# Transformer block with attention and experts: the first two stages reordered over three DMA queues

## What is computed

```python
s = layernorm(attention(xn) + bo + xn) * gamma + beta      # 16 heads of 16
# scores = (q k^T + rel_q + rel_k) / sqrt(D); rel_q, rel_k from a table of distances
y = xn + n1 + (n1 @ mix_w + mix_b);  n1 = layernorm(xn)*g1+be1
g = silu(y + sum of the best two of 8 experts on layernorm(y)*g2+be2)
```

## Time and profile before

| | |
|---|---|
| median of 3 runs | 2211.05 us (2209.01 to 2214.07) |
| the profiled execution | 2215.61 us, its span 2213.7 us |
| mean granted clock of PE | 0.869 |
| `project` | 0 to 165.6 us |
| `route` | 165.6 to 464.5 us |
| `experts` | 464.5 to 1494.3 us |
| `attention` | 1494.3 to 2213.7 us; PE busy 589.5, DVE 546.9, ACT 532.2 us |

### The profile page before, as it was taken

One profiled execution on the slowest core, in us unless ns is written; L12 is line 12 of the kernel. 1 busy time (PEld: TensorE's weight loads), 2 busy tenths in 40 slices (PEclk: granted clock), 3 DMA queues, 4 the chain that ended last, 5 costly groups with the idle time before them and its releaser, 6 DMA issues. The chain is left out here.

```text
span 2213.7 us, 32508 instructions
## 1 busy us (share of the span) xinstructions
PE 1652.7 (75%) x11192; PEld 1210.2 (55%) x11192; DVE 1144.9 (52%) x2980; ACT 1020.5 (46%) x2057; POOL 664.0 (30%) x711
## 2 busy tenths in 40 slices
PE   5536353027889788987989798976898998899881
PEld 2213133026777677876777687863555555555550
DVE  5722636503333244443323344435888888888870
ACT  3534110012434233333433234326878878888870
POOL 2560025821111111111111111105206446437435
PEclk9767575568999899999999899987999999999995
DMA  4445474778899999998999999969989899899851
GB/s 158 128 138 154 139 248 119 209 193 252 289 302 316 313 330 309 321 303 281 308 283 314 334 322 308 312 231 332 304 262 303 278 324 314 264 327 315 277 173 38
DMA packets 247731, 576.91 MB, mean 261 GB/s; under 512 B 40016, under 2 KB 86608, under 8 KB 246160
## 3 DMA queue, kind: packets, MB, share of 16 engines
q1 hardware_dynamic: 204160, 426.81, 58.0%
q0 software_dynamic: 43408, 148.04, 21.3%
HBM read 371.27 MB, written 203.42 MB: 260 GB/s over the span
## 5 line engine op out<-in xcount | busy, mean ns | idle before, releaser
L953 DVE TENSOR_TENSOR rel_out<-rl,rel_tile 128x1024 f32<-128x1024 f32 x256 | 307.5, 1221 | 240.7 <-PE rl L1005 169.9
L1220 ACT ACTIVATE scores<-scores,row_least 128x512 f32<-128x512 f32 x512 | 365.6, 717 | 25.1 <-DVE row_least L1253 24.5
L1253 DVE CUSTOM_DVE_ANT_1 scores<-sc,rq 128x512 f32<-128x512 f32 x512 | 336.7, 687 | 36.5 <-issue 35.2
L930 ACT COPY rel_tile<-rl 128x1024 f32<-128x1024 f32 x256 | 249.5, 1017 | 228.6 <-PE rl L1005 195.6
L1354 PE MATMUL pt<-ident,scores 128*128 128x128 f32 x2048 | 328.6, 285 | 30.8 <-DVE probsT L1259 15.9
L1026 PE MATMUL up<-rowsT,w 128*128 128x256 f32 x1280 | 326.5, 400 | 3.5 <-DMA w<-in_w 3.5
L1039 PE MATMUL dn<-w,hid 128*128 128x256 f32 x1280 | 326.2, 400 | 0.0
L938 ACT ACTIVATE hid<-up,b 128x256 f32<-128x256 f32 x320 | 134.1, 470 | 390.9 <-PE up L1026 390.2
L1354 PEld LDWEIGHTS pt<-ident,scores 128*128 128x128 f32 x2048 | 256.3, 147 | 105.6 <-DVE probsT L1259 52.9
L1026 PEld LDWEIGHTS up<-rowsT,w 128*128 128x128 f32 x1280 | 241.0, 199 | 32.1 <-issue 3.9
L1039 PEld LDWEIGHTS dn<-w,hid 128*128 128x128 f32 x1280 | 241.8, 199 | 28.4
(11 more groups left out here) (182 smaller groups left out, 1735.7 us busy)
## 6 DMA issues: line engine op xcount, KB each, us to landing
scratch_rel<-rel_out SPq DMA_DIRECT2D x256, 512.0 KB, 8.6
rq<-scratch_rel SPq DMA_DIRECT2D x256, 512.0 KB, 5.9
w<-in_w POOLq DMA_DIRECT2D x80, 1024.0 KB, 11.0
krows_sb<-scratch_stack SPq DMA_DIRECT2D x768, 64.0 KB, 5.3
scratch_parts<-part SPq DMA_DIRECT2D x96, 128.0 KB
by_head<-scratch_parts SPq DMA_DIRECT2D x16, 768.0 KB, 5.8
scratch_stack<-by_row SPq DMA_DIRECT2D x4, 3072.0 KB, 22.9
qrows_sb<-scratch_stack SPq DMA_DIRECT2D x192, 64.0 KB, 8.6
```

The lines of the kernel that those rows point to most:

```text
L930: nc.scalar.copy(both[:, :, u * UN:(u + 1) * UN], rl[r][:].rearrange("p a (b l) -> p l (a b)", l=TILE)).then_inc(s_kc, 1)
L953: nc.vector.tensor_tensor(out[n % SRING][:], rl[r][:].rearrange("p a (b s) -> p (a b) s", s=TILE), both[:, u * UN:(u + 1) * UN], ALU.add). ...
L1220: nc.scalar.activation(sm[j][:, i], sm[j][:, i], ACT.Exp, bias=least[:, j, i:i + 1], scale=-1.0, accum_out=es[:, g // 2 % 2, i, 2 * j + g ...
L1253: nc.vector.tensor_tensor_reduce(sm[j][:, i].rearrange("p (c s) -> p c s", c=LT), sc[i % 2][:].rearrange("p (c s) -> p c s", c=LT), rq[j][ ...
```

## The change

- `project`: the ring of parts has three places. ACT makes only part 0; `rest` works per output `c` on DVE straight from PSUM (add the bias, subtract part 0), and PE may reuse the output when `rest` has read it. DVE's normalization is cut into `statistics`, `roots`, `applied` and `second_scale`, which alternate with the rests; the tables are split last. PE turns batch 0 first and makes the constants after the products of batch 0. POOL no longer adds `bo` or `cvec`. SP stores plain `xn` and loads four small tables for `route`.
- `route`: `va` is stored from ACT's queue and `x1` from POOL's, SP keeps loads and stores of the repacking. POOL adds `cvec` to `xn` (`shifted`). DVE clears `va`. The copies alternate: ACT has (0, 0), (0, 2), (0, 4), (0, 6), (1, 0), (1, 3), (1, 6), DVE the nine others; those of the second half stand behind `place_pair(3)` on DVE and behind `exponents(3)` on ACT. The first stack store stands behind the loads (1, 0) and (1, 1) on SP.
- `experts`: the eight query pieces of the first row of tiles are requested one at a time, each ahead of a key piece.
- `attention`: `xo` is reloaded from plain `xn`, and `bo` is added by a product of a row of ones with `bo`, one more call per 128 rows.

```diff
+PRING = 3
+ZRING = 2
...
+        qk = [sb(f"qk_rest{i}", [P, 4, S]) for i in range(2)]
+        part = [[sb(f"part{i}_{k}", [P, 4, S], BF16) for k in range(PARTS)] for i in range(PRING)]
...
+            sp.dma_start(keep["tri"][:], t["tri"]).then_inc(s_ahead, 16)
+            sp.dma_start(keep["rw"][:], t["router_w"].rearrange("(k p) n -> p k n", p=P)).then_inc(s_ahead, 16)
+            sp.dma_start(keep["first_row"][:], t["first_row"].partition_broadcast(P)).then_inc(s_ahead, 16)
+            sp.dma_start(keep["turn_no"][:], t["turn_no"].partition_broadcast(P)).then_inc(s_ahead, 16)
+
+            def store_xn(b):
+                sp.wait_ge(s_xn, b + 1)
+                sp.dma_start(t["xn"][b * S:(b + 1) * S].rearrange("(p t) e -> p t e", t=ST), xn[:, b * ST:(b + 1) * ST]).then_inc(s_xs[b], 16)
+
+            store_xn(0)
+            store_xn(1)
             for b in range(B):
-                par = b % 2
-                sp.wait_ge(s_xb, b + 1)
-                sp.dma_start(t["xnbo"][b * S:(b + 1) * S].rearrange("(p t) e -> p t e", t=ST), xb[par][:]).then_inc(s_xs[par], 16)
                 for k, done in enumerate((s_p0, s_p1, s_p2)):
                     sp.wait_ge(done, 4 * (b + 1) if k == 0 else b + 1)
                     for c in range(4):
                         at = b * H + (c % 2) * (H // KC)
                         dst = t["parts"][c // 2 * PARTS + k, :, at:at + H // KC].rearrange("d h s -> h d s")
-                        sp.dma_start(dst, part[par][k][:, c]).then_inc(s_ps[par], 16)
-            for i in range(2):
-                sp.wait_ge(s_xs[i], 16 * B // 2)
-                sp.wait_ge(s_ps[i], 16 * 4 * PARTS * B // 2)
+                        sp.dma_start(dst, part[b % PRING][k][:, c]).then_inc(s_ps[b % PRING], 16)
+                if b + 2 < B:
+                    store_xn(b + 2)
+            sp.wait_ge(s_ahead, 16 * 4)
+            for b in range(B):
+                sp.wait_ge(s_xs[b], 16)
+            for i in range(PRING):
+                sp.wait_ge(s_ps[i], 16 * 4 * PARTS * len(range(i, B, PRING)))
 
         @block.gpsimd
...
             for b in range(B):
-                par, own = b % 2, slice(b * ST, (b + 1) * ST)
-                pool.wait_ge(s_vec, 2)
-                pool.wait_ge(s_xn, b + 1)
-                after(pool, s_xs[par], 16 * (b // 2))
-                nc.gpsimd.tensor_tensor(xb[par][:], xn[:, own], over_tiles(bo[:], ST), ALU.add).then_inc(s_xb, 1)
                 pool.wait_ge(s_p1, b + 1)
-                after(pool, s_ps[par], 16 * 4 * PARTS * (b // 2))
-                nc.gpsimd.tensor_tensor(part[par][2][:], qk[par][:], part[par][1][:], ALU.subtract).then_inc(s_p2, 1)
-                pool.wait_ge(s_t, (b + 1) * KC)
-                pool.wait_ge(s_xb, b + 1)
-                nc.gpsimd.tensor_tensor(xn[:, own], xn[:, own], over_tiles(cvec[:], ST), ALU.add).then_inc(s_xc, 1)
+                after(pool, s_ps[b % PRING], 16 * 4 * PARTS * (b // PRING))
+                nc.gpsimd.tensor_tensor(part[b % PRING][2][:], qk[b % 2][:], part[b % PRING][1][:], ALU.subtract).then_inc(s_p2, 1)
...
-            def take_products(b):
-                par = b % 2
-                for c in range(4):
-                    act.wait_ge(s_qk, b * 4 + c + 1)
-                    if c == 0:
-                        after(act, s_p2, b - 1)
-                    nc.scalar.activation(in_order(qk[par][:, c]), by_row(prod[c][:]), ACT.Identity, bias=bqk[:, c:c + 1]).then_inc(s_q32, 1)
-                    if c == 0:
-                        after(act, s_ps[par], 16 * 4 * PARTS * (b // 2))
-                    nc.scalar.activation(in_order(part[par][0][:, c]), by_row(prod[c][:]), ACT.Identity, bias=bqk[:, c:c + 1]).then_inc(s_p0, 1)
+            def first_part(b, c):
+                dst = part[b % PRING][0][:, c].rearrange("e (p t) -> e p t", t=ST)
+                act.wait_ge(s_qk, b * 4 + c + 1)
+                if c == 0:
+                    after(act, s_ps[b % PRING], 16 * 4 * PARTS * (b // PRING))
+                nc.scalar.activation(dst, in_order(prod[c][:]), ACT.Identity, bias=bqk[:, c:c + 1]).then_inc(s_p0, 1)
 
             def second_part(b):
-                act.wait_ge(s_r, b + 1)
-                nc.scalar.copy(part[b % 2][1][:], qk[b % 2][:]).then_inc(s_p1, 1)
+                act.wait_ge(s_r, 4 * (b + 1))
+                nc.scalar.copy(part[b % PRING][1][:], qk[b % 2][:]).then_inc(s_p1, 1)
 
             take_turned(0)
             for b in range(B):
-                take_products(b)
+                first_part(b, 0)
+                first_part(b, 1)
+                if b:
+                    second_part(b - 1)
+                first_part(b, 2)
                 if b + 1 < B:
                     take_turned(b + 1)
-                if b:
-                    second_part(b - 1)
+                first_part(b, 3)
             second_part(B - 1)
...
+            def rest(b, c):
+                turned = prod[c][:].rearrange("e (t p) -> e p t", t=ST)
+                dve.wait_ge(s_p0, 4 * b + c + 1)
+                if c == 0:
+                    after(dve, s_p2, b - 1)
+                nc.vector.scalar_tensor_tensor(qk[b % 2][:, c].rearrange("e (p t) -> e p t", t=ST), turned, bqk[:, c:c + 1],
+                                               part[b % PRING][0][:, c].rearrange("e (p t) -> e p t", t=ST),
+                                               ALU.add, ALU.subtract).then_inc(s_r, 1)
...
+            statistics(0, 0)
+            statistics(0, 1)
+            roots()
+            applied(0, 0)
+            applied(0, 1)
+            second_scale(0)
+            dve.wait_ge(s_wqk, 16 * 3)
+            for p in range(B // 2):
+                more = p + 1 < B // 2
+                rest(2 * p, 0)
+                if more:
+                    statistics(p + 1, 0)
+                rest(2 * p, 1)
+                if more:
+                    statistics(p + 1, 1)
+                rest(2 * p, 2)
+                rest(2 * p, 3)
+                if p == 0:
+                    dve.wait_ge(s_once, 1)
+                    nc.vector.tensor_tensor(cvec[:], once[:, 0], rows[:, 0], ALU.add).then_inc(s_vec, 1)
+                    nc.vector.tensor_tensor(bo[:], once[:, 1], rows[:, 1], ALU.add).then_inc(s_vec, 1)
+                if more:
+                    roots()
+                rest(2 * p + 1, 0)
+                if more:
+                    applied(p + 1, 0)
+                rest(2 * p + 1, 1)
+                rest(2 * p + 1, 2)
+                if more:
+                    applied(p + 1, 1)
+                rest(2 * p + 1, 3)
+                if more:
+                    second_scale(p + 1)
             dve.wait_ge(s_tabs, 16 * 3)
             split_table(tabq, 0)
-            rest(4)
             split_table(tabk, 1)
-            for b in range(5, B):
-                rest(b)
 
...
+            turn(0)
             pe.wait_ge(s_wqk, 16 * 3)
-            turn(0)
             for b in range(B):
-                products(b)
+                for c in range(3):
+                    product(b, c)
                 if b + 1 < B:
                     turn(b + 1)
+                product(b, 3)
+                if b == 0:
+                    pe.wait_ge(s_w, 16 * 5)
+                    pe.wait_ge(s_setup, 2 + KC)
+                    for i, w in enumerate((mix, wo)):
+                        for k in range(KC):
+                            last = nc.tensor.matmul(once[:, i], spread[:, i, k], w[:, k], start=(k == 0), stop=(k == KC - 1))
+                    last.then_inc(s_once, 1)
...
+        BY_DVE = ((0, 1), (0, 3), (0, 5), (0, 7), (1, 1), (1, 2), (1, 4), (1, 5), (1, 7))
+        BY_ACT = tuple((half, b) for half in range(2) for b in range(B) if (half, b) not in BY_DVE)
+
+        def repack_done(eng, half, b):
+            if (half, b) in BY_DVE:
+                eng.wait_ge(s_bd, BY_DVE.index((half, b)) + 1)
+            else:
+                eng.wait_ge(s_ba, BY_ACT.index((half, b)) + 1)
...
+            for b in range(B):
+                load(0, b)
             load(1, 0)
             load(1, 1)
-            store_back(4)
-            store_back(5)
-            store_back(6)
-            store_back(7)
+            store_rows(0)
             for b in range(2, B):
                 load(1, b)
             store_rows(1)
-            for i in range(2):
-                sp.wait_ge(s_vs[i], 16 * B // 2)
-            sp.wait_ge(s_x1, 16 * B)
             sp.wait_ge(s_bs, 16 * LT)
...
+            def shifted(b):
+                own = slice(b * ST, (b + 1) * ST)
+                nc.gpsimd.tensor_tensor(xn[:, own], xn[:, own], over_tiles(cvec[:], ST), ALU.add).then_inc(s_xc, 1)
+
+            def store_x1(b):
+                pool.wait_ge(s_x2, (b + 1) * ST)
+                pool.dma_start(t["x1"][b * S:(b + 1) * S].rearrange("(p t) e -> p t e", t=ST), xn[:, b * ST:(b + 1) * ST]).then_inc(s_x1, 16)
+
+            for b in range(B):
+                shifted(b)
+                if 1 < b < 6:
```

(82 more changed lines are left out.)

175 lines of the change are left out of this document (65 added, 110 removed).

## The result

| | before | after | forecast |
|---|---|---|---|
| median | 2210.03 us (4 runs) | 2177.52 us (4 runs, 2170.55 to 2181.86) | 2114 (2075 to 2160) |
| profiled execution | 2215.61 us, span 2213.7 | 2177.89 us, span 2176.3 | |
| `project` | 165.6 | 128.2 | 106 |
| `route` | 298.9 | 290.2 | 265 |
| `experts` | 1029.8 | 1020.7 | 1017 |

A forecast was written before the change was run, and what follows sets the result against it. The first two stages were taken as bound by order and waits, with no engine full. Project -60, route -34, experts -13 and attention +10 made -97 us, giving a median of 2114 us, range 2075 to 2160.

The forecast's parts named there:

- four signs of being wrong: `project` over 120 us, `rest` over 1 us beside POOL, `route` ending on POOL instead of the stores, attention over 15 us longer.
- Project, start: PE's first product in `project` at 17 us instead of 24.54, 7.5 us earlier, with the constants behind batch 0.
- Project, pace: 9.3 us per batch in `project`, 74 for eight; bounds 8.7 and 12.5.
- rival 1: POOL and DVE block each other in `project`: pace 12.5, stage 132, total 2140; chance 0.27 shared by three rivals.
- Project, end: Last rest, second and third part, four stores and landing in `project` take 13.5 us, with the table splitting hidden beside them.
- Rival 6: No change in time, which would need the front stages to be bound by transfers; chance 0.02.
- Route, until the first stack store: In `route`, first slots at T+64, third at T+157, first stack stores out at T+162, counted from the stage's start.
- Route, stack landing: In `route`, the first stack stores take 28 us to land, at T+190.
- rival 2: In `route`, stack store pairs take 34 us, loads 10 instead of 5.8; total 2139; chance 0.27 shared by three rivals.
- Route, end: `route` ends with its stack stores at T+265; POOL's path, clearings 9 us then 15 more, ends just under, at T+261.
- Experts: At the start of `experts`, spreading query requests between key pieces shortens PE's wait: -13 us (-20 to -4).
- Attention: 32 bias calls of two PE instructions, about 0.23 us each, cost 0 to 15 us in `attention`; taken as +10.

The follow-up runs named there:

- the mend: POOL's third part of batches 0, 2 and 4 also waits until the next pair is normalized, against the changed kernel; ratio 0.9813 to the kernel before, `project` 117.9 us.

## Why the prediction was right or wrong

The mechanisms that the change was built on came. The profiled stages together exceed the forecast ones by 59 us, and 47 of these lie in `project` and `route`. The steps that failed there are the overlap of POOL's third part with DVE's normalization, which the sum put at nothing, and POOL's path at the end of `route`, which it took too short. Three of the four signs of being wrong came too: `project` over 120 us, the end of `route` on POOL, and attention over 15 us longer. The fourth, `rest` at over 1 us beside POOL, did not.

- **Project, start:** right. First product at 16.6 us, forecast 17. Of this the constants' move is worth 3 us, the turning's the rest.
- **Project, pace:** this step failed. The prediction asked of `rest` whether POOL blocks it, and answered rightly that it doesn't. It did not ask the same of the second piece of DVE work that the change puts beside POOL's third part, the normalization, which reads and writes SBUF. There the four instructions took 5.1 us instead of 1.4, with PE and ACT in a chain behind them. That is the mechanism of rival 1. That its price of 12.5 us per batch lies so near the 12.2 measured is luck: it counted 4.1 us of blocked DVE in every batch, but 3.7 to 3.8 were blocked once per pair. The rest is PE's lower clock behind its waits, which neither the sum nor the rival had. In the kernel before, all 32 took 0.41 us on average; they lay between POOL's instructions, at 58.43 us for example, where POOL rested from 55.6 to 63.0. The Trainium skill (SBUF — State Buffer, "Who interferes with whom") names `tensor_scalar` beside copies and casts among those that can take the port pair that DVE shares with POOL; the runs agree (1.4 against 5.1 us for four), and the prediction had cited that section only for copies and casts.
- **Project, end:** failed too. It summed computation and counted SP's stores as 8.7 us per batch, from the earlier trace rows. That row has the time of the issues, and the `xn` store was counted as one more issue, not as a transfer. Streaming, a batch of them takes 9.4 to 10.5 us with the `xn` store. An estimate from rows agrees: 12 stores of 128 KB at 190 GB/s make 8.3 us, and 512 KB of `xn` at the 343 GB/s reached in its slices 1.5 us more. With the third part behind the normalization, SP is a batch behind: its last 24 issues run from 96.4 to 113.7 us, while ACT has made the last second part at 96.5. That is why the kernels with the mend take 115.4 to 120.1 us and not 106. Rival 6 was turned down with a DMA share of 0.44; with these stores, 0.60 was as far as it went.
- **Route, until the first stack store:** right in sum (T+163.6, forecast 162), partly by luck: the first scatter came 5.8 us late, at T+69.8 instead of 64, and the pairs made up 3.8 of it, 44.7 us apart instead of 46.6.
- **Route, stack landing:** mis-sized. 28 us is right for the stores alone. Scatters of pairs 2 and 3, which the forecast itself put at the same time, make it 38; rival 2 had the mechanism, at 34. Its slower loads did not come: the second half took 45.3 us, forecast 45.6.
- **Route, end:** this step failed. The clearings were counted at 9 us, from the kernel before, where they stood in POOL's stream behind scatters. Now POOL waits for the rows, and 16 take 20.2 us. Then 20.2 more pass until the stage ends, not 15. The prediction gave 4 us between this path and the stores and did not ask which of the two it knew worse; putting four small DVE steps earlier was worth 11.6 us.
- **Experts:** 13 us forecast, 9 in the profiled pair, about 7 on average, by the mechanism forecast. Single executions lie up to 13 us apart.
- **Attention:** mis-sized. Each call costs 0.62 us, not two times 0.23, so up to 20 us and not 15 at full weight; 17.8 came in the profile, 13 by leaving it out. One row costs as much as 128: 444 ns on average for 256 columns, where the old products take 400.
- **Rivals:** 1 came by its mechanism and nearly at its price, 2 in part; the range's upper end had allowed for the two only in part. Rivals priced one at a time hid that both rest on POOL: on what DVE does beside its third part in `project`, and on its scatters beside the stores in `route`.

## What to carry to other kernels

When work moves beside an engine that shares a port with its own, every instruction that is moved has to be asked, by its operands, and not only the new ones. When a step is made last in order, count what runs behind it on its slowest engine, with the fetch of each operand that was hidden before; a path within a few us of the one that is thought to end the stage needs its own working. A wait of PE can cost more than its length, since its clock may fall behind it. A low DMA share is no proof of room: look at what a stream of the same packets reaches when nothing else holds it.

## What the runs showed of the hardware that was not expected

- A stage whose last transfers are POOL's ends some 8 us after its last packet. In the changed kernel the queues are empty from about 410 to 418.4 us, and in the kernel before from 457 to 464.5. In the two runs with scatters held back they are empty from about 407.5 to 415.87 and from about 396.5 to 404.52. Where the clearings were done early, the block ended 0.2 us behind the last stack store. What POOL or its queue does in these 8 us no row shows, and it was not tried apart.
- POOL's issue of a scatter takes 0.97 us, but 4.5 to 6.4 when a DVE copy of `by_row` starts beside it: it is held for about the length of the copy.
- Stores of 128 KB parts alone reached 176 to 192 GB/s at a DMA share of 0.53 to 0.55, and some 205 at 0.60 with an `xn` store of 512 KB per batch among them, from one issuing engine as from two.
- Behind waits of 5.6 and 6.2 us PE's granted clock was 0.50 for the next 4 to 5 us, and products took 3.2 to 3.6 us instead of 1.88. Behind waits of 1.80 and 2.88 us it was 1.00, but behind one of 2.87 us 0.57.
